# Cross-attention kernel with two layers: context rows of five units normalised on GpSimd, one context block loaded earlier, ternary weights made in the first pass

## The chip, the cores and the metric

The kernel runs on one core of a Trainium2 chip. The metric is the device time of one execution in microseconds (us). Five engines work side by side, each with its own instruction stream and tied to the others by semaphores alone: PE (TensorE, matmuls), DVE (VectorE), ACT (ScalarE), POOL (GpSimd) and SP (SyncE), which here issues every DMA.

## What is computed

Eight batch elements, each with 56 query rows of width 128 and 1500 context rows of width 128; 16 heads of width 8.

```python
q = _ln(latents); x = latents + _mha(q, q)                 # self-attention
kv = _ln(tokens)                                           # tokens = ctx_1024, layernormed
x = x + _mha(_ln(x), kv)                                   # cross-attention, layer 0
x = _fuse_moe(x)                                           # 8 experts, top 2
# layer 1: cross-attention on the context as it is, with ternary weights
gamma = mean(|W|); Wq = clip(round(W / (gamma + 1e-5)), -1, 1) * gamma
x = x + softmax(q @ k.T * SCALE) @ v @ bit_quant(Wo).T + bo
```

## The kernel before, in words

The work is a self-attention, then pass 0 (cross-attention of layer 0), the router and the experts, then pass 1 (cross-attention of layer 1). A pass has eight **units**, one per batch element, and eight **windows**, one per unit. Window n has 12 steps (STEPS). In it PE does the scores of unit n (L1149), the score tiles of unit n+1 (and in window 0 six of its own) whose row maxima DVE takes (`reduce_tile`, L791), the values (L1185), the keys of unit n+2 (`project_k`, L1091, steps 0 to 2), the values' projection of unit n+1 (`project_v`, L1101, steps 4 to 6) and, in pass 0 for n = 0 to 4, the transposes of the normalised context of unit n+3 (`transpose_ctx`, L1080, steps 9, 10, 11). The order of the work is written out by hand, and every engine keeps to its own order.

**Score tiles.** A tile is one 96x112 by 96x500 matmul (L1170) into one of two banks, and DVE reduces it over its 500 columns (L791). PE may begin tile j only when DVE has reduced tile j-2 (`wait(pe, sm_red, n.count(TILES, j + 1 - banks))`). STEP_TILES puts 3, 3, 3, 2, 2, 2, 2, 2, 1, 1, 2, 1 tiles into the steps of a window.

**Context of pass 0.** A block of 1500 context rows is loaded by SP into one of two buffers `cx` (`load_ctx`, L332), as 125 partitions by 12 chunks by 128. In window n DVE takes the statistics of unit n+3 (`ctx_stats`, L763, three chunks in each of steps 1 to 4, the first behind a wait for the load), in step 5 it aggregates them (`ctx_aggregate`, L770 and L773), POOL raises the variance to the power -0.5 (`ctx_rstd`, L464), and in steps 7, 8 and 9 DVE normalises four chunks each in place (`ctx_normalise`, L779: a TENSOR_SCALAR with a mean and a factor per partition). PE transposes chunk by chunk in steps 9 to 11, one third at a time, behind `cn_ready`. Units 0, 1 and 2 have these steps before window 0.

**The keys' split.** ACT writes kf and the first bf16 part (L564, L565), POOL the rest (`k_rest`, L471), DVE the second part (L786), POOL the third (L476). POOL's window is `k_parts(n + 2)` with `ctx_rstd(n + 3)` at its end. SP restacks the parts into kst (`restack`, L378, 6 DMAs for each half).

**SP's queue.** Ahead of window 0: `load_ctx` of units 0, 1 and 2, both halves of `restack(u0)`, the weights of experts 0 and 1 (L351, L352), `load_qall(0)` (L360: 6 DMAs, each behind the part of the split queries it carries), `shift(u0, 0)` (L385), `restack(u1, 0)`. Window n: `load_ctx(n+3)`, `restack(n+1, 1)`, `shift(n, 1)`, `restack(n+2, 0)`, `shift(n+1, 0)`. `load_ctx(n)` waits for the transposes of unit n-2 (`xt_full`).

**The start of pass 0 on DVE.** `split_q(0)` (L749 to L757), then the ternary weights (L936 to L951: 12 TENSOR_SCALAR-like instructions and two whole-tile ones, 128 partitions each), then `start_pass(0)`, whose first instruction is `place_q(u0, 0)` (L815), behind a wait for all six qall DMAs. Pass 1 has the same start without the ternary weights. `place_q` comes again in step 1 and in step 10 of every window. The weights' result (`wq_ready`) is first used by PE after window 7 of pass 0.

Of the kernel before, what the change touches and what calls it, by code (L numbers as in the profile page):

```python
# [26 lines left out]
ALU = mybir.AluOpType  # L27
# [5 lines left out]
B, L, D, T = 8, 56, 128, 1500  # L33
H, DH = 16, 8
E, DFF = 8, 512
EPS = 1e-5
# [14 lines left out]
HSTEP = STEPS // 2  # L51
TPAD = KC * (NCH - 1) + 128
THIRD = T // 3
CPT = NCH // 3
# [95 lines left out]
def build_kernel(nc, x_in, ctx_in, ctxT_in, watt_in, vec_in, rows_in, rwT_in, w1T_in, w2T_in, b2_in,  # L150
                 ident_in, mask_in, out):
    with ExitStack() as ctx:
# [21 lines left out]
        watt = sb("watt", [128, 3, 4, 128])  # L174
# [24 lines left out]
        cmv = sb("cmv", [KC, NCH, 2])  # L199
# [121 lines left out]
        def _(sp):  # L321
# [5 lines left out]
            def load_ctx(n):  # L327

                if n.it is not None or n.c >= 2:
                    sp.wait_ge(xt_full, (n + -2).count(3, 3))  # L330
                src = ctx_in[bass.ds(n.u, 1)].rearrange("a (p c) d -> (a p) c d", c=NCH)
                sp.dma_start(cx[n.par][:], src).then_inc(ld_ctx[n.par], 16)  # L332
# [17 lines left out]
            def load_expert(e, j):  # L350
                sp.dma_start(w1s[j], w1T_in[bass.ds(e, 1)].rearrange("a i f -> (a i) f")).then_inc(ld_exp[j], 16)  # L351
                sp.dma_start(w2s[j], w2T_in[bass.ds(e, 1)].rearrange("a f c d -> (a f) c d")).then_inc(ld_exp[j], 16)  # L352
# [29 lines left out]
            def shift(n, half):  # L382

                sp.wait_ge(mx_evac, n.count(2, half + 1))
                sp.dma_start(qst[n.par][SROWS:KROWS, 4 * half:4 * half + 4, :], mrow[:, half, :]  # L385
                             ).then_inc(shift_loaded[half][n.par], 16)

            def window(n):
                if n.s == 0 and (n + 3).exists():
                    load_ctx(n + 3)  # L390
                if (n + 1).exists():
                    restack(n + 1, 1)
                shift(n, 1)
                if (n + 2).exists():
                    restack(n + 2, 0)
                if (n + 1).exists():
                    shift(n + 1, 0)
                if n.s == 1 and (n + 3).exists():
                    load_xT(n + 3)

# [2 lines left out]
            load_ctx(Unit(0, None, 2))  # L403
            restack(u0, 0)
            restack(u0, 1)
            load_expert(0, 0)
            load_expert(1, 1)
            load_qall(0)
# [28 lines left out]
        @block.gpsimd  # L437
        def _(pool):
            nc.gpsimd.memset(half_neg[:], -0.5)
            nc.gpsimd.memset(euler[:], float(np.e))  # L440
            nc.gpsimd.memset(mean_w[:], 1.0 / (D * D))
            nc.gpsimd.memset(ones_rows[:], 1.0)
            nc.gpsimd.memset(ones_row[:], 1.0)
            for s in range(2):
                last = nc.gpsimd.memset(kst[s][0:SROWS, :, T:TPAD], 0.0)
            last.then_inc(padded, 1)

            def spread_q(b):

                pool.wait_ge(sa_q, 1)  # L450
                wait(pool, sa_sm_full, b - 1)
                nc.gpsimd.tensor_tensor(
                    qbd[:, b % 2], q_sa[:, L * b:L * (b + 1)].unsqueeze(1).broadcast_to([128, H, L]),
                    mask[:, 0:H].unsqueeze(2).broadcast_to([128, H, L]), ALU.mult).then_inc(sa_qbd, 1)

            def token_rstd(n):

                pool.wait_ge(xvar_ready, n + 1)
                nc.gpsimd.tensor_tensor(xrstd[:], xvar[:], half_neg[0:TP, 0:TT], ALU.pow).then_inc(xrstd_ready, 1)  # L459

            def ctx_rstd(n):

                pool.wait_ge(cvar_ready, n.count(1, 1))
                nc.gpsimd.tensor_tensor(crstd[:], cvar[:], half_neg[0:KC, 0:NCH], ALU.pow).then_inc(crstd_ready, 1)  # L464

            def k_rest(n, i):

                wait(pool, k3_done, n.count(3, i - 2))
                pool.wait_ge(k_evac, n.count(6, 2 * i + 2))
                c = slice(THIRD * i, THIRD * (i + 1))  # L470
                nc.gpsimd.tensor_tensor(kr[:, c], kf[:, c], ksplit[n.par][:, 0, c], ALU.subtract).then_inc(kr_done, 1)  # L471

            def k_third_part(n, i):
                pool.wait_ge(k2_done, n.count(3, i + 1))
                c = slice(THIRD * i, THIRD * (i + 1))
                nc.gpsimd.tensor_tensor(ksplit[n.par][:, 2, c], kr[:, c], ksplit[n.par][:, 1, c],  # L476
                                        ALU.subtract).then_inc(k3_done, 1)

            def gates_exp():

                pool.wait_ge(gexp_in, 1)
                nc.gpsimd.tensor_tensor(gates[:], euler[:], lg[:], ALU.pow).then_inc(gexp_done, 1)

            def k_parts(n, ln_unit, between=None):
                k_rest(n, 0)
                k_rest(n, 1)
                if between is not None:
                    between()
                k_third_part(n, 0)
                k_rest(n, 2)  # L490
                k_third_part(n, 1)
                k_third_part(n, 2)
                if ln_unit is not None:
                    ctx_rstd(ln_unit)

            def window(n):
                ln_unit = n + 3 if n.s == 0 and (n + 3).exists() else None
                if (n + 2).exists():
                    k_parts(n + 2, ln_unit)

            pool.wait_ge(padded, 1)
            token_rstd(0)
            u0, u1 = Unit(0, None, 0), Unit(0, None, 1)
            pool.wait_ge(ld_mask, 16)
            spread_q(0)
            spread_q(1)
            for i in range(SA_STEPS):
                if i + 2 < B:
                    spread_q(i + 2)
                if i == 0:  # L510
                    ctx_rstd(u0)
                if i == 3:
                    ctx_rstd(u1)
                if i == 8:
                    ctx_rstd(u0 + 2)

                for kind, unit, third in SA_PIECES.get(i - 1, ()):
                    if kind == "k":
                        k_rest(u0, third)
                for kind, unit, third in SA_PIECES.get(i - 3, ()):  # L520
                    if kind == "k":
                        k_third_part(u0, third)
            token_rstd(1)
            k_parts(u1, None)
            run_windows(0, window)
            token_rstd(2)
            v0 = Unit(1, None, 0)
            k_parts(v0, None, gates_exp)
            token_rstd(3)
            k_parts(v0 + 1, None)  # L530
            run_windows(1, window)


# [178 lines left out]
        def _(dve):  # L712
# [119 lines left out]
            def add_projection(n):  # L832
# [2 lines left out]
                nc.vector.tensor_tensor(xt[:], xt[:], PO[0:TP, :].rearrange("p (t d) -> p t d", t=TT), ALU.add  # L835
                                        ).then_inc(x_added, 1)

            def window(n):
                nxt, k_unit = n + 1, n + 2
                ln_unit = n + 3 if n.s == 0 and (n + 3).exists() else None  # L840
# [2 lines left out]
                for k in range(STEPS):  # L843
# [19 lines left out]
                            max_parts(nxt, 0)  # L863
                    if 0 <= k - K_STEP - 1 < 3 and k_unit.exists():
                        k_second_part(k_unit, k - K_STEP - 1)
                    if ln_unit is not None:
                        if k in (1, 2, 3, 4):
                            ctx_stats(ln_unit, range(3 * (k - 1), 3 * k))
                        if k == 5:
                            ctx_aggregate(ln_unit)  # L870
                        if k in (7, 8, 9):
                            ctx_normalise(ln_unit, (k - 7,))

            every = range(NCH)
            u0, u1 = Unit(0, None, 0), Unit(0, None, 1)
# [55 lines left out]
            token_gain(1)  # L931
            split_q(0)


            dve.wait_ge(gam_ready, 1)
            nc.vector.tensor_scalar(thr[:, 0], gam[:], EPS, 0.5, ALU.add, ALU.mult)  # L936
            nc.vector.tensor_scalar(thr[:, 1], gam[:], EPS, -0.5, ALU.add, ALU.mult).then_inc(thr_ready, 1)
            dve.wait_ge(thr_ready, 1)
            for w in range(4):
                nc.vector.tensor_scalar(wt[:, 0, w], watt[:, 2, w], thr[:, 0, w:w + 1], None, ALU.is_gt)  # L940
                last = nc.vector.tensor_scalar(wt[:, 1, w], watt[:, 2, w], thr[:, 1, w:w + 1], None, ALU.is_lt)
            last.then_inc(tern1, 1)
            dve.wait_ge(tern1, 1)
            nc.vector.tensor_tensor(wt[:, 0], wt[:, 0], wt[:, 1], ALU.subtract).then_inc(tern2, 1)
            dve.wait_ge(tern2, 1)
            for w in range(4):
                last = nc.vector.scalar_tensor_tensor(out=wt[:, 1, w], in0=wt[:, 0, w], scalar=gam[:, w:w + 1],
                                                      in1=watt[:, 2, w], op0=ALU.mult, op1=ALU.subtract)
            last.then_inc(tern3, 1)
            dve.wait_ge(tern3, 1)  # L950
            nc.vector.tensor_tensor(watt[:, 2], watt[:, 2], wt[:, 1], ALU.add).then_inc(wq_ready, 1)  # L951

            def start_pass(s):
                first = Unit(s, None, 0)
# [513 lines left out]
```

## Time and profile before

| | us |
|---|---|
| runs shown | 637.69, 639.55, 640.61; median 639.55 |
| profiled execution, its own time | 638.79 |
| its span | 637.0 |
| busy in the span: PE | 544.5 (85%) |
| DVE | 425.6 (67%) |
| ACT | 326.7 (51%) |
| POOL | 152.7 (24%) |
| chain that ended last | PE 45%, DVE 23%, issue 21%, DMA 4%, POOL 3% |

The profile is of one execution; its own time is its span and 1.79 us around it. Busy shares are averages over stages with different limits, so a stage is read by its own rows. "Idle before" in a row of the trace is the time that an engine sat still ahead of the instruction, with what released it. The granted clock of PE is 1.00 at 2.4 GHz and 0.50 at 1.2 GHz.

### The profile page before, as it was taken

What the parts mean: (1) busy time and instruction counts of PE and PEld (TensorE: products, weight loads), DVE (VectorE), ACT (ScalarE), POOL (GpSimd) and SP (SyncE); (2) the same over time, 40 slices, a digit from 0 to 9 for tenths busy, and PEclk for the clock granted to TensorE, in tenths of its full rate; (3) what the DMA queues carried; (4) which work ended last, traced back from release to release, by engine and by line L of the source; (5) the groups of instructions that cost most, each with busy time, mean ns of one, the idle gap of its engine ahead of it and who ended that gap; (6) DMA issues with size and microseconds to landing.
All of it is one profiled execution on the core that took longest, in us unless ns stands there. A gap on an engine that the chain in (4) does not pass through costs nothing.

```text
span 637.0 us, 16158 instructions
## 1 busy us (share of the span) xinstructions
PE 544.5 (85%) x6582; PEld 383.9 (60%) x6582; DVE 425.6 (67%) x1090; ACT 326.7 (51%) x495; POOL 152.7 (24%) x128
## 2 busy tenths in 40 slices
PE   0699838589999999999967989468999999999996
PEld 0587515266766667676745767234666767667674
DVE  5667478679998999977224302569787687786730
ACT  0165214356666576765743333215566567676573
POOL 1554212313241524300015100223041240421000
PEclk9899668889999999999997989878999999999998
DMA  5010733434436353342200642026536436353300
GB/s 154 32 50 1 164 92 69 126 88 110 132 74 172 72 139 75 75 99 50 100 1 1 170 108 66 9 84 146 137 80 175 121 77 168 88 137 75 74 3 15
DMA packets 25338, 57.44 MB, mean 90 GB/s; under 512 B 4660, under 2 KB 8876, under 8 KB 25268
## 3 DMA queue, kind: packets, MB, share of 16 engines
q1 hardware_dynamic: 25268, 56.45, 34.6%
q8 instruction: 51, 0.84, 0.5%
q14 instruction: 19, 0.16, 0.1%
HBM read 17.81 MB, written 0.23 MB: 28 GB/s over the span
## 4 chain that ended last, share of the span: by engine, by line
PE 45%; DVE 23%; issue 21%; DMA 4%; POOL 3%; ACT 2%; SPq 2%; DVEq 0%; POOLq 0%; ACTq 0%
DVE mxp L791 11%; PE SM L1170 10%; PE PO L1185 9%; PE ST L1149 6%; PE MI L1101 6%; DMA cx<-in_ctx 3%; PE MI L1091 3%; DVE cx L779 3%; DVE qst L815 2%; PE MI L1125 2%; PE SM L1257 2%; DVE ksplit L786 1%; DVE cstat L763 1%; PE SM L1125 1%; DVE xn L732 1%
## 5 line engine op out<-in xcount | busy, mean ns | idle before, releaser
L791 DVE TENSOR_REDUCE mxp<-SM 112x1 f32<-112x500 f32 x364 | 235.2, 673 | 60.5 <-PE SM L1170 59.1
L593 ACT ACTIVATE PT<-ST 128x896 f32<-128x896 f32 x192 | 171.1, 911 | 49.7 <-PE ST L1149 49.1
L1170 PE MATMUL SM<-kst,qst 96*112 96x500 bf16 x364 | 143.1, 407 | 24.7 <-DVE mxp L791 24.1
L1149 PEld LDWEIGHTS ST<-qst,kst 98*128 98x128 bf16 x1536 | 95.0, 100 | 32.6 <-issue 9.7
L1149 PE MATMUL ST<-qst,kst 98*128 98x112 bf16 x1536 | 108.5, 215 | 1.2 <-DMA qst<-mrow 1.2
L471 POOL TENSOR_TENSOR kr<-kf,ksplit 128x500 f32<-128x500 f32 x48 | 56.1, 1170 | 184.4 <-ACT ksplit L565 184.3
L1185 PE MATMUL PO<-PT,vaug 125*32 125x112 f32 x3072 | 96.5, 264 | 2.1 <-ACT PT L593 1.5
L1170 PEld LDWEIGHTS SM<-kst,qst 96*112 96x112 bf16 x364 | 46.8, 131 | 66.9 <-DVE mxp L791 55.2
L1185 PEld LDWEIGHTS PO<-PT,vaug 125*32 125x32 f32 x3072 | 70.5, 110 | 24.5 <-issue 14.9
L577 ACT ACTIVATE vaug<-MI 125x512 f32<-125x512 f32 x48 | 28.7, 598 | 79.4 <-PE MI L1101 79.4
L476 POOL TENSOR_TENSOR ksplit<-kr,ksplit 128x500 bf16<-128x500 f32 x48 | 54.5, 1135 | 53.4 <-DVE ksplit L786 53.4
L1101 PE MATMUL MI<-watt,xT 128*125 128x128 f32 x384 | 56.9, 294 | 0.1
L1101 PEld LDWEIGHTS MI<-watt,xT 128*125 128x125 f32 x384 | 49.1, 197 | 8.9 <-issue 5.0
L564 ACT ACTIVATE kf<-MI,vec 128x500 f32<-128x500 f32 x42 | 28.5, 678 | 40.0 <-PE MI L1091 40.0
L1091 PE MATMUL MI<-xT,watt 128*128 128x500 f32 x84 | 45.9, 629 | 0.0
L699 ACT ACTIVATE moe<-ST,vec 128x448 f32<-128x448 f32 x32 | 20.1, 634 | 35.5 <-PE ST L1368 35.0
L1379 PEld LDWEIGHTS SM<-moe 128*112 128x112 f32 x256 | 31.9, 181 | 9.8 <-issue 8.9
L1023 DVE SCALAR_TENSOR_TENSOR xt<-SM,gates,xt 112x128 f32<-112x128 f32 x32 | 9.0, 343 | 40.4 <-PE SM L1379 40.4
L459 POOL TENSOR_TENSOR xrstd<-xvar,half_neg 112x4 f32<-112x4 f32 x4 | 4.0, 1010 | 127.1 <-DVE xvar L729 127.1
L1368 PE MATMUL ST<-hT,moe 128*128 128x448 f32 x64 | 31.0, 590 | 2.2 <-DMA moe<-in_w2T 2.2
L1379 PE MATMUL SM<-moe 128*112 128x128 f32 x256 | 32.6, 276 | 0.0
L779 DVE TENSOR_SCALAR cx<-cx,cmv,crstd 125x128 f32<-125x128 f32 x96 | 28.6, 366 | 2.7 <-POOL crstd L464 2.7
(129 smaller groups left out, 555.4 us busy)
## 6 DMA issues: line engine op xcount, KB each, us to landing
kst<-ksplit SPq DMA_DIRECT2D x192, 187.5 KB, 3.8
cx<-in_ctx SPq DMA_DIRECT2D x8, 750.0 KB
xT<-in_ctxT SPq DMA_DIRECT2D x8, 750.0 KB, 4.6
moe<-in_w1T SPq DMA_DIRECT2D x8, 256.0 KB, 2.9
moe<-in_w2T SPq DMA_DIRECT2D x8, 256.0 KB, 3.3
qall<-qsplit SPq DMA_DIRECT2D x12, 112.0 KB, 2.3
watt<-in_watt SPq DMA_DIRECT2D x1, 768.0 KB, 5.8
qst<-mrow SPq DMA_DIRECT2D x32, 1.8 KB
```

The source lines that it names most:

```text
L471: nc.gpsimd.tensor_tensor(kr[:, c], kf[:, c], ksplit[n.par][:, 0, c], ALU.subtract).then_inc(kr_done, 1)
L476: nc.gpsimd.tensor_tensor(ksplit[n.par][:, 2, c], kr[:, c], ksplit[n.par][:, 1, c], ALU.subtract).then_inc(k3_done, 1)
L593: nc.scalar.activation(PT[:, k % PTB], ST[:, k % 2, :, 0:4 * PC], ACT.Exp, scale=SCALE).then_inc(exp_done, 1)
L779: last = nc.vector.tensor_scalar(cx[n.par][:, c], cx[n.par][:, c], cmv[:, c, 0:1], crstd[:, c:c + 1], ALU.subtract, ALU.mult)
L791: nc.vector.tensor_reduce(mxp[:, j // 3, j % 3:j % 3 + 1], tile_bank(j, banks), AX.X, ALU.max).then_inc(sm_red, 1)
L1091: mm(bank[:, 0:THIRD], watt[:, n.s + 1, 1], xT[n.par][:, THIRD * i:THIRD * (i + 1)], start=True, stop=True).then_inc(kp_full, 1)
L1101: last = mm(MI[0:KC, D * c:D * (c + 1)], xT[n.par][:, at:at + KC], watt[:, n.s + 1, 2], start=True, stop=True)
L1149: last = mm(ST[:, k % 2, cc, PC * p:PC * (p + 1)], kst[n.par][:, 4 * half + p, at:at + 128], qst[n.par][:, 4 * half + p], start=True, stop ...
L1170: mm(tile_bank(j, banks), qst[n.par][0:SROWS, j // 3], kst[n.par][0:SROWS, j // 3, at:at + THIRD], start=True, stop=True).then_inc(sm_full, 1)
L1185: last = mm(PO[32 * p:32 * p + 32, PC * half:PC * (half + 1)], vaug[n.par][:, c, at:at + 32], PT[0:KC, k % PTB, cc, PC * p:PC * (p + 1)], ...
L1368: mm(ST[:, c // 2, c % 2, 0:N], w1s[j][:, D * c:D * (c + 1)], hT[:], start=True, stop=True).then_inc(fc1_full, 1)
L1379: last = mm(SM[0:TP, j, D * t:D * (t + 1)], h1[:, c, TP * t:TP * (t + 1)], w2s[j][:, c], start=(c == 0 and t == 0), stop=(c == CPE - 1), s ...
```

## The change

1. For units 3 to 7, the 12 normalising TENSOR_SCALARs leave DVE (steps 7, 8, 9 of windows 0 to 4) and go to POOL, right behind `ctx_rstd` of the same unit. In step 5 DVE now waits, before it overwrites the statistics, until POOL has normalised the unit before (units 4 to 7).
2. `load_ctx(n+4)` stands at the end of SP's window n, where `load_ctx(n+3)` stood at the head of window n, and `load_ctx` of unit 3 goes ahead of the experts' weights and of `load_qall(0)`.
3. The ternary weights go from the start of pass 0 to window 5 of pass 0, on DVE behind step 6 and ahead of step 7.

```diff
@@ SP @@
             def window(n):
-                if n.s == 0 and (n + 3).exists():
-                    load_ctx(n + 3)
                 if (n + 1).exists():
                     restack(n + 1, 1)
                 shift(n, 1)
                 if (n + 2).exists():
                     restack(n + 2, 0)
                 if (n + 1).exists():
                     shift(n + 1, 0)
+                if n.s == 0 and (n + 4).exists():
+                    load_ctx(n + 4)
...
             load_ctx(Unit(0, None, 2))
             restack(u0, 0)
             restack(u0, 1)
+            load_ctx(Unit(0, None, 3))
             load_expert(0, 0)
             load_expert(1, 1)
             load_qall(0)
@@ POOL @@
+            def ctx_normalise(n):
+                pool.wait_ge(crstd_ready, n.count(1, 1))
+                for i in range(3):
+                    for c in range(CPT * i, CPT * (i + 1)):
+                        last = nc.gpsimd.tensor_scalar(cx[n.par][:, c], cx[n.par][:, c], cmv[:, c, 0:1],
+                                                       crstd[:, c:c + 1], ALU.subtract, ALU.mult)
+                    last.then_inc(cn_ready, 1)
             def window(n):
                 ln_unit = n + 3 if n.s == 0 and (n + 3).exists() else None
                 if (n + 2).exists():
                     k_parts(n + 2, ln_unit)
+                if ln_unit is not None:
+                    ctx_normalise(ln_unit)
@@ DVE, in the loop over the steps k of a window @@
+                    if n.s == 0 and n.c == B - 3 and k == HSTEP:
+                        ternary_weights()
                     if ln_unit is not None:
                         if k in (1, 2, 3, 4):
                             ctx_stats(ln_unit, range(3 * (k - 1), 3 * k))
                         if k == 5:
+                            if ln_unit.it is not None or ln_unit.c > 3:
+                                dve.wait_ge(cn_ready, (ln_unit + -1).count(3, 3))
                             ctx_aggregate(ln_unit)
-                        if k in (7, 8, 9):
-                            ctx_normalise(ln_unit, (k - 7,))
@@ DVE, between split_q(0) and start_pass(0) @@
-            (the ternary weights, L935 to L951, now in ternary_weights())
```

## Rows read from the trace of the kernel before

**Rows 1.** Busy time by stretch: from, to, length, each engine; then PEclk, DMA share, GB/s.

```profile
111.92:151.06 39.14, 30.29 (x364) 20.91 (x363) 29.00 (x85) 18.56 (x29) 8.90 (x8) 0.87 0.46 122
436.85:464.90 28.05, 25.69 (x352) 17.06 (x352) 23.53 (x48) 17.10 (x26) 7.12 (x7) 1.00 0.60 146
151.06:166.57 15.51, 14.33 (x193) 10.19 (x191) 14.61 (x48) 9.19 (x14) 8.10 (x7) 1.00 0.31 73
166.57:178.90 12.33, 11.91 (x176) 8.54 (x175) 11.13 (x30) 9.65 (x16) 1.36 (x2) 1.00 0.61 163
490.45:505.38 14.93, 14.18 (x193) 10.15 (x191) 11.50 (x24) 9.07 (x14) 6.37 (x6) 1.00 0.35 81
505.38:515.99 10.61, 10.45 (x164) 7.14 (x163) 8.29 (x18) 7.60 (x13) 0.39 (x1) 1.00 0.70 184
```

**Rows 2.** Timeline of DVE in window 0 of pass 0: start, duration, idle before.

```profile
121.02 0.68 DVE L763 BATCH_NORM_STATS2 cstat<-cx 125x6 f32<-125x128 f32 x3 [5.51 <-DMA cx<-in_ctx]
```

**Rows 3.** Timeline of SP's queue, 60 to 190 us and 404 to 420 us.

```profile
76.55 0.99 SPq L351 DMA_DIRECT2D moe<-in_w1T  x1
86.24 3.78 SPq L360 DMA_DIRECT2D qall<-qsplit  x6
109.32 0.78 SPq L332 DMA_DIRECT2D cx<-in_ctx  x1
...
412.06 3.78 SPq L360 DMA_DIRECT2D qall<-qsplit  x6
```

**Rows 4.** Timeline of DVE at the starts of pass 0 and of pass 1.

```profile
87.88 0.16 DVE L936 TENSOR_SCALAR thr<-gam 128x4 f32<-128x4 f32 x1
92.35 0.46 DVE L815 TENSOR_SCALAR qst<-qall,member 96x224 bf16<-96x224 bf16 x2
...
417.65 0.46 DVE L815 TENSOR_SCALAR qst<-qall,member 96x224 bf16<-96x224 bf16 x2 [3.88 <-DMA qall<-qsplit]
```

**Rows 5.** Stretches as in rows 1: SP's queue running dry, and the end of a context load.

```profile
82.00:84.00 2.00, 1.07 (x5) 0.59 (x6) 0.74 (x1) 0.00 (x0) 0.00 (x0) 0.90 0.16 60
118.00:120.00 2.00, 0.00 (x0) 0.00 (x0) 0.00 (x0) 0.00 (x0) 0.52 (x1) 1.00 0.31 121
```

**Rows 6.** Timeline of PE in window 1 of pass 0: first and third group of transposes.

```profile
169.99 0.59 PE L1080 MATMUL MI<-ident,cx 125*128 125x125 f32 x4
...
173.79 0.59 PE L1080 MATMUL MI<-ident,cx 125*128 125x125 f32 x4
```

**Rows 7.** Timeline of POOL, window 1 and start of window 2 of pass 0.

```profile
165.27 2.27 POOL L464 TENSOR_TENSOR crstd<-cvar,half_neg 125x12 f32<-125x12 f32 x1 [4.30 <-DVE cvar L773]
178.51 1.13 POOL L471 TENSOR_TENSOR kr<-kf,ksplit 128x500 f32<-128x500 f32 x1 [10.97 <-ACT ksplit L565]
```

**Rows 8.** Groups of POOL by line and shape: busy, mean ns, idle before.

```profile
L471 POOL TENSOR_TENSOR kr<-kf,ksplit 128x500 f32<-128x500 f32 x48 | 56.1, 1170 | 184.4 <-ACT ksplit L565 184.3
...
L452 POOL TENSOR_TENSOR qbd<-qf,mask 128x896 f32<-128x896 f32 x8 | 13.5, 1688 | 22.0 <-PE SM L1257 12.5 <-DVE qf L885 9.5
...
L441 POOL MEMSET mean_w<- 128x128 f32 x1 | 0.2, 204 | 0.0
```

**Rows 9.** Timeline of DVE in window 5 of pass 0, steps 6 to 8.

```profile
277.43 0.68 DVE L791 TENSOR_REDUCE mxp<-SM 112x1 f32<-112x500 f32 x1 [1.51 <-PE SM L1170]
278.53 1.87 DVE L791 TENSOR_REDUCE mxp<-SM 112x1 f32<-112x500 f32 x3 [0.42 <-PE SM L1170]
```

**Rows 10.** Timeline of PE in the same steps.

```profile
279.26 0.42 PE L1170 MATMUL SM<-kst,qst 96*112 96x500 bf16 x1 [0.16 <-DVE mxp L791]
```

**Rows 11.** PE after an idle time among the experts (timeline); two stretches at low clock (as rows 1).

```profile
372.45 3.60 PE L1368 MATMUL ST<-hT,moe 128*128 128x448 f32 x6 [2.19 <-DMA moe<-in_w2T]
...
122.30:131.50 9.20, 8.82 (x70) 6.17 (x71) 5.79 (x15) 2.56 (x4) 2.27 (x2) 0.51 0.02 8
373.70:377.00 3.30, 3.30 (x10) 2.05 (x9) 0.00 (x0) 1.87 (x3) 0.00 (x0) 0.51 0.01 2
```

**Rows 12.** Timeline of DVE at the start of window 2 of pass 0.

```profile
178.82 1.08 DVE L815 TENSOR_SCALAR qst<-qall,member 96x224 bf16<-96x224 bf16 x2
```

More of the change, by code:

```diff
@@ L836, in add_projection, with ternary_weights @@
                                         ).then_inc(x_added, 1)
+            def ternary_weights():
+                dve.wait_ge(gam_ready, 1)
+                nc.vector.tensor_scalar(thr[:, 0], gam[:], EPS, 0.5, ALU.add, ALU.mult)
+                nc.vector.tensor_scalar(thr[:, 1], gam[:], EPS, -0.5, ALU.add, ALU.mult).then_inc(thr_ready, 1)
+                dve.wait_ge(thr_ready, 1)
+                for w in range(4):
+                    nc.vector.tensor_scalar(wt[:, 0, w], watt[:, 2, w], thr[:, 0, w:w + 1], None, ALU.is_gt)
+                    last = nc.vector.tensor_scalar(wt[:, 1, w], watt[:, 2, w], thr[:, 1, w:w + 1], None, ALU.is_lt)
+                last.then_inc(tern1, 1)
+                dve.wait_ge(tern1, 1)
+                nc.vector.tensor_tensor(wt[:, 0], wt[:, 0], wt[:, 1], ALU.subtract).then_inc(tern2, 1)
+                dve.wait_ge(tern2, 1)
+                for w in range(4):
+                    last = nc.vector.scalar_tensor_tensor(out=wt[:, 1, w], in0=wt[:, 0, w], scalar=gam[:, w:w + 1],
+                                                          in1=watt[:, 2, w], op0=ALU.mult, op1=ALU.subtract)
+                last.then_inc(tern3, 1)
+                dve.wait_ge(tern3, 1)
+                nc.vector.tensor_tensor(watt[:, 2], watt[:, 2], wt[:, 1], ALU.add).then_inc(wq_ready, 1)
             def window(n):
@@ L932, in _ @@
             split_q(0)
[L935 to L951, printed above, removed]
             def start_pass(s):
```

## The prediction

> **What bounds the kernel now.** I read the share of busy time first, and it only says where to look: PE is busy for 85% of the span and DVE for 67%, over stages that differ. The edits touch three places: the start of pass 0, windows 0 to 4 of pass 0 and window 5. So I cut the timeline at events that both passes have and compared the passes, since a window of pass 1 is one of pass 0 without the context's layernorm. The cuts are `place_q` in step 1 and the transposes back of `on` (L1137, step 7).
>
> Window 1 of pass 0 takes 15.51 + 12.33 = 27.84 us, a middle window of pass 1 14.93 + 10.61 = 25.54 us [rows 1]. PE is busy for 26.24 of the 27.84 us and 24.63 of the 25.54 us. A window is bound by PE, with short waits for DVE in between, although DVE is busy for 25.7 us in pass 0. The layernorm costs 2.30 us of a window: 0.58 in steps 1 to 7 (where DVE takes statistics) and 1.72 in steps 7 to 1 (where it normalises and PE transposes).
>
> Window 0 of pass 0 takes 39.14 us and that of pass 1 28.05 us [rows 1]. DVE stood for 5.51 us until the block of unit 3 had landed [rows 2]: its load was issued at 109.32 us, behind the restack of unit 1's first half [rows 3]. With PE idle, the granted clock then fell, and 9.2 us ran at 0.51 (the 1.2 GHz level) [rows 11].
>
> **Edit 2, the loads.** From unit 4 on the position in SP's queue is the one before: the end of window n is the head of window n+1, with nothing between. Only the load of unit 3 moves, from 109.32 us to about 76.6 us, ahead of the experts' weights [rows 3]. Its condition, the transposes of unit 1, is met by then. It lands some 30 us before DVE asks for it, so the wait goes. What is won: window 0 has 39.14 - 28.05 = 11.09 us more than its twin in pass 1. Of that 2.30 is the layernorm as in window 1, and some 1.0 I leave for statistics, because here DVE has six more tiles and no slack in steps 1 to 3. The rest, 7.8 us (the wait of 5.51 and 2.3 of low clock), goes. Next late is DVE's work in steps 1 to 3, as in pass 1. Bounds: 5.5 (the clock stays low for some other cause) to 9.
>
> The moved load has a price at the start. Behind it stand `load_qall(0)`'s six DMAs, for which DVE's first `place_q` waits. At the end of a context load the DMA share is 0.31 and the rate 121 GB/s [rows 5]: 5 of 16 engines carry it, and 750 KB take them 6.3 us. The queue now runs dry at about 83 us (share 0.16) [rows 5], so those five would be free at about 89 us, as the last of the qall DMAs is issued (86.24 + 3.78 us) [rows 3]. I count it with edit 3.
>
> **Edit 3, the ternary weights.** Taking them from the start looks like 92.35 - 87.88 = 4.47 us of DVE [rows 4]. But `place_q` also waits for qall. In pass 1, where no ternary weights stand there, it begins 417.65 - 412.06 = 5.59 us after the first qall issue, with a wait of 3.88 us [rows 3, 4]; in pass 0 it begins 92.35 - 86.24 = 6.11 us after it. So at most 0.52 us is won, the rest was cover for the DMA. The moved load may take that back: I put -0.2, between -0.5 and +1.5.
>
> In window 5 the 4.47 us stand as one block between the reduces of two tiles, and PE has two banks. The reduce of 277.43 us ends at 278.11, the block at 282.5, the next reduce at 283.2. PE begins the tile after next at 279.26 us, released by just that reduce, now the first of the three at 278.53 us [rows 9, 10]. It would begin at 283.25: +4.0 us. PE runs in order, so the values and scores behind it wait too, and DVE's idle time later in the window gives nothing back. And the clock: an idle time of 2.19 us among the experts was followed by 3.3 us at 0.51, the idle time of window 0 by 9.2 us [rows 11]. At half the clock a stretch loses at most half its length, and window 0 lost about 2.3 of 9.2 us, a quarter: 0.8 to 4.6 us, I take 2.2. Together +6.2 us. Bounds: +1.5 (PE finds other cover) to +8.5.
>
> **Edit 1, the normalising.** Off DVE go 12 instructions a window, but what that gives is what PE waited for them. Of the 1.72 us in steps 7 to 1, PE's three groups of transposes take 1.3 (0.59 us each, overlapping the next by some 0.15) [rows 6] and stay. Left is 0.4 us a window, five windows: -2.0 us. Bounds 0 and -3.
>
> On POOL, 12 TENSOR_SCALARs of 125x128 come behind the power, which ends at 165.27 + 2.27 = 167.54 us [rows 7]. PE wants the first third at 169.99 and the last at 173.79 us [rows 6], 173.4 once the 0.4 is gone. So one may take (173.4 - 167.54) / 12 = 0.49 us. No row shows it. From below: a 128x128 MEMSET at 204 ns. From above: a line through the two TENSOR_TENSORs, 1170 ns at 500 columns and 1688 at 896, which gives 0.68 us at 128 columns [rows 8]. The 500-column one scaled by columns gives 0.30. This one reads one tensor, not two, and so stands nearer to that; I take 0.35 us, 4.2 us for twelve, ready at 171.7 us: hidden, with 1.7 us to spare. At 0.68 us it is 2.3 us late a window. POOL's next work begins at 178.51 us [rows 7], so neither the keys' split nor DVE's new wait in step 5 is reached.
>
> **The sum**, against the profiled execution (638.79 us: span 637.0 and 1.79 around it): -7.8 - 0.2 + 6.2 - 2.0 = -3.8, that is 635.0 us. It is 0.76 below the median of the runs shown, so 635.7 us.
>
> **A page that speaks against edit 1.** `place_q` on DVE took 1.08 us for two at 178.82 us, while POOL worked from 178.51 to 179.64 [rows 7, 12]; a pair elsewhere takes 0.46 [rows 4]. The Trainium skill, Perfetto Trace Analysis, section Optimizing Scalar/DVE Operations, says that work moved between GpSimd and VectorE may not help as they share an SBUF port; this row agrees for `place_q`. By it edit 1 would give nothing, 637.7 us; the sum keeps its 2.0, because what DVE runs in steps 6 to 9 are reduces that read PSUM.
>
> **The rivals.** (a) Window 5 is cheap: PE's stall stays 4.0 but the clock holds (633.5), or DVE's block is covered (629.5). For it: PE is dense around it. Against: the two rows on the clock. Chance 0.2. (b) Slower than before: POOL's instruction price becomes the bound. Place: the transposes in steps 9 to 11 of five windows. At 0.68 us each is 12 x 0.68 - 5.86 = 2.3 us late, +11.5: 647.2 us. It outweighs the rest from 5 x (12p - 5.86) = 3.8, p = 0.55 us. For it: the line through the two rows; against: one input, and the small MEMSETs that show little fixed cost. Chance 0.15, half of it between 0.49 and 0.6 us, near no change. (c) DVE finds no relief, by POOL's share of the port: 637.7 us, chance 0.1. (d) The moved load holds back qall by 1.5 us or the clock stays low in window 0: 638 us. Chance 0.1. (e) The change does not do what it says, the block of unit 3 still lands late: it needs only the transposes of unit 1, far behind by then; with edit 3's price it would end 4 us above before. Chance 0.02. The forecast has 0.43.
>
> **The numbers.** Some 0.5% (3.2 us) is what a measurement of this kernel can tell from no change: faster means below 636.3 us. Most of the forecast's own spread (633 to 638) lies below, and (a) all of it: 0.57. Within: the forecast's upper part, (c), (d) and the middle of (b): 0.3. Slower: 0.13. The range 630 to 640.5 leaves out the fully covered window 5 and (b) beyond 0.57 us.
>
> **What would show it.** Right: no wait of DVE for `cx` in window 0, which takes 31 us; clock 1.00 from about 111 us on; windows 1 to 4 at 27.4 us; `place_q` at 5.6 to 6.5 us after the first qall issue; in window 5 an idle time of PE of 4 us behind the ternary weights and a stretch at 0.5 after it; POOL's TENSOR_SCALAR near 0.35 us. Wrong: PE waiting in L1080 for POOL in steps 9 to 11, or a window 5 as long as before.

## The result, and the profile after

| | us |
|---|---|
| before, median of 4 runs | 640.08 (637.69 to 642.92) |
| changed kernel, median of 4 runs | 666.39 (660.20 to 667.74) |
| ratio, 95% interval | 1.039 (1.031 to 1.047) |
| profiled execution: its own time, span | 667.74, 665.9 |
| busy in the span | PE 559.8 (84%), DVE 412.2 (62%), POOL 200.2 (30%) |

The change costs 3.9%, where 0.6% less was forecast. 666.39 us lies outside the range given (630 to 640.5). Now and then an execution runs at a lower clock and takes some per cent longer; the ratios leave such a one out, here a single one (652.43 us, of the kernel with edit 1 undone), which only that kernel's median counts.

Busy time by stretch of the changed kernel, columns as in rows 1. Each of the first four is a window (0, 1, 2 and 5), from its `place_q` of step 1 to the next window's; the fifth is a piece of window 2.

```profile
115.68:151.36 35.68, 30.31 (x364) 20.65 (x363) 26.70 (x72) 18.56 (x28) 17.91 (x20) 0.88 0.49 118
151.36:184.25 32.89, 28.03 (x367) 19.64 (x366) 23.05 (x65) 19.00 (x29) 18.90 (x20) 0.95 0.37 95
184.25:218.25 34.00, 29.14 (x367) 20.39 (x366) 23.05 (x65) 19.09 (x29) 18.89 (x20) 0.90 0.37 92
286.41:317.35 30.94, 25.80 (x352) 18.07 (x350) 24.02 (x57) 16.15 (x24) 6.46 (x6) 0.89 0.25 57
...
209.50:216.50 7.00, 5.98 (x49) 4.07 (x50) 1.84 (x6) 2.17 (x4) 0.87 (x2) 0.52 0.72 166
```

DVE's busy time in a window fell from 25.7 to 23.05 us, as the edit meant, and the window went from 27.84 [rows 1] to 34.00 us. The two profiled spans, cut at events that both have, differ so:

| stretch | before | after | difference |
|---|---|---|---|
| start to the first qall issue | 86.24 | 87.90 | +1.66 |
| to the first `place_q` | 6.11 | 7.97 | +1.86 |
| to window 0, step 1 | 19.57 | 19.81 | +0.24 |
| window 0 | 39.06 | 35.68 | -3.38 |
| windows 1 to 4 | 111.72 | 135.05 | +23.33 |
| window 5 | 24.79 | 30.94 | +6.15 |
| the rest | 349.51 | 348.55 | -0.96 |
| span | 637.0 | 665.9 | +28.9 |

The first line is no effect of the change: its code ahead of that point is the one before but for one DMA issued at 78.65 us, and the other kernels, with or without that DMA, show 85.87 to 88.62 us.

POOL in window 2, its timeline (start, duration, count), answering to rows 7:

```profile
198.56 2.29 POOL L465 TENSOR_TENSOR crstd<-cvar,half_neg 125x12 f32<-125x12 f32 x1 [4.31 <-DVE cvar L785]
200.95 9.42 POOL L502 TENSOR_SCALAR cx<-cx,cmv,crstd 125x128 f32<-125x128 f32 x12
```

Twelve instructions take 9.42 us, 0.785 us each. PE in the same window, its timeline:

```profile
204.23 0.62 PE L1096 MATMUL MI<-ident,cx 125*128 125x125 f32 x4 [0.78 <-POOL cx L502]
...
207.42 0.62 PE L1096 MATMUL MI<-ident,cx 125*128 125x125 f32 x4 [1.06 <-POOL cx L502]
...
210.52 1.07 PE L1096 MATMUL MI<-ident,cx 125*128 125x125 f32 x4 [1.66 <-POOL cx L502]
...
212.68 1.72 PE L1201 MATMUL PO<-PT,vaug 125*32 125x112 f32 x32
```

Each third of the transposes waits for POOL, 3.5 us in all; in window 0 it is some 2 us (16.0 us over the five windows). POOL's longer work holds up nothing else: its next instruction, for the keys' split, began after 7.58 us of idle time, and DVE did not stand in step 5. With the third wait the four transposes take 1.07 us where they took 0.62, and the values behind them 1.72 us: the clock has fallen to the 1.2 GHz level, and 7 us run at 0.52.

Window 5, PE's timeline around the ternary weights, answering to rows 10:

```profile
302.26 0.56 PE L1165 MATMUL ST<-qst,kst 98*128 98x112 bf16 x8
306.94 0.67 PE L1186 MATMUL SM<-kst,qst 96*112 96x500 bf16 x1 [4.12 <-DVE mxp L803]
307.54 1.72 PE L1201 MATMUL PO<-PT,vaug 125*32 125x112 f32 x32
```

An idle time of 4.12 us, and low clock behind it. At the start DVE's first `place_q`, and what SP issued ahead of it (timelines of DVE and SP, answering to rows 4 and 3):

```profile
95.87 0.46 DVE L827 TENSOR_SCALAR qst<-qall,member 96x224 bf16<-96x224 bf16 x2 [6.24 <-DMA qall<-qsplit]
```

```profile
78.65 0.83 SPq L332 DMA_DIRECT2D cx<-in_ctx  x1
...
87.90 3.77 SPq L360 DMA_DIRECT2D qall<-qsplit  x6
```

DVE waits 6.24 us for the qall DMAs: the 4.47 us of ternary weights that covered such a wait are gone, and the DMAs land later, 7.97 us after the first issue where the start of pass 1 showed 5.59.

### The profile page after: what moved, and what is told of

Same layout as the page of the kernel before. It is cut to its first block, busy times and chain, and to the rows that moved or that the text cites. A ratio compares the mean times of both kernels' runs of the same rounds, so it can differ in the third digit from the quotient of the medians.

```text
span 665.9 us, 16158 instructions
## 1 busy us (share of the span) xinstructions
PE 559.8 (84%) x6582; PEld 395.7 (59%) x6582; DVE 412.2 (62%) x1030; ACT 328.1 (49%) x495; POOL 200.2 (30%) x188
## 4 chain that ended last, share of the span: by engine, by line
PE 44%; issue 20%; DVE 18%; POOL 11%; DMA 3%; ACT 1%; SPq 1%; DVEq 0%; ACTq 0%; POOLq 0%
DVE mxp L803 9%; PE SM L1186 9%; PE PO L1201 8%; POOL cx L502 7%; PE ST L1165 6%; PE MI L1117 5%; PE MI L1107 4%; POOL crstd L465 2%; PE MI L1141 2%; DVE qst L827 2%; PE SM L1273 2%; DMA cx<-in_ctx 2%; DVE ksplit L798 1%; PE MI L1096 1%; DVE cstat L775 1%
## 5 line engine op out<-in xcount | busy, mean ns | idle before, releaser
L1186 PE MATMUL SM<-kst,qst 96*112 96x500 bf16 x364 | 145.6, 415 | 20.9 <-DVE mxp L803 20.5
L1165 PEld LDWEIGHTS ST<-qst,kst 98*128 98x128 bf16 x1536 | 96.9, 102 | 34.6 <-issue 11.9
L1165 PE MATMUL ST<-qst,kst 98*128 98x112 bf16 x1536 | 110.6, 217 | 1.1 <-DMA qst<-mrow 1.1
L1201 PE MATMUL PO<-PT,vaug 125*32 125x112 f32 x3072 | 100.7, 271 | 2.1 <-ACT PT L605 1.5
L1201 PEld LDWEIGHTS PO<-PT,vaug 125*32 125x32 f32 x3072 | 74.0, 113 | 25.7 <-issue 17.3
L1107 PE MATMUL MI<-xT,watt 128*128 128x500 f32 x84 | 49.0, 668 | 0.0
L502 POOL TENSOR_SCALAR cx<-cx,cmv,crstd 125x128 f32<-125x128 f32 x60 | 47.0, 799 | 0.5
L1395 PEld LDWEIGHTS SM<-moe 128*112 128x112 f32 x256 | 31.2, 177 | 9.3 <-issue 8.3
L564 ACT ACTIVATE xT<-MI,vec 128x500 f32<-128x500 f32 x24 | 18.4, 767 | 31.5 <-PE MI L1096 31.5
L1096 PE MATMUL MI<-ident,cx 125*128 125x125 f32 x96 | 17.4, 312 | 18.1 <-POOL cx L502 16.0
```

What stands on the lines that cost most here:

```text
L502: last = nc.gpsimd.tensor_scalar(cx[n.par][:, c], cx[n.par][:, c], cmv[:, c, 0:1], crstd[:, c:c + 1], ALU.subtract, ALU.mult)
L1107: mm(bank[:, 0:THIRD], watt[:, n.s + 1, 1], xT[n.par][:, THIRD * i:THIRD * (i + 1)], start=True, stop=True).then_inc(kp_full, 1)
L1165: last = mm(ST[:, k % 2, cc, PC * p:PC * (p + 1)], kst[n.par][:, 4 * half + p, at:at + 128], qst[n.par][:, 4 * half + p], start=True, stop ...
L1186: mm(tile_bank(j, banks), qst[n.par][0:SROWS, j // 3], kst[n.par][0:SROWS, j // 3, at:at + THIRD], start=True, stop=True).then_inc(sm_full, 1)
L1201: last = mm(PO[32 * p:32 * p + 32, PC * half:PC * (half + 1)], vaug[n.par][:, c, at:at + 32], PT[0:KC, k % PTB, cc, PC * p:PC * (p + 1)], ...
L1395: last = mm(SM[0:TP, j, D * t:D * (t + 1)], h1[:, c, TP * t:TP * (t + 1)], w2s[j][:, c], start=(c == 0 and t == 0), stop=(c == CPE - 1), s ...
```

## The experiments

The kernel before was measured again beside each group of kernels, and every ratio is against those runs. What was open: whether POOL's price, the time of one of its instructions, made the windows long (theory P), or the moved load (L), or the ternary weights (S), and what the low clock adds.

**Edit 1 undone.** The changed kernel with the normalising back on DVE, and without DVE's wait in step 5.

```diff
-                if ln_unit is not None:
-                    ctx_normalise(ln_unit)
...
                             ctx_aggregate(ln_unit)
+                        if k in (7, 8, 9):
+                            ctx_normalise(ln_unit, (k - 7,))
```

> The changed kernel with the normalising of units 3 to 7 back on DVE (edit 1 undone, edits 2 and 3 kept). Theory P (POOL's price of 0.79 us an instruction makes the transposes late, and the idle time drops the clock): windows 1 to 4 return from 33 to 34 us to 27.9 us, window 0 to about 31 us, window 5 stays near 31 us; 638 us (636 to 641). Rival L (what costs is the moved load, through the DMA queue and the clock at the start): it stays above 655 us. Rival S (the ternary weights in window 5 are the larger loss): above 650 us.

Measured: 641.63 us (median of ten), ratio 1.002 (1.000 to 1.005). The stretches of windows 0, 1 and 5:

```profile
114.41:146.96 32.55, 28.58 (x364) 19.66 (x365) 29.24 (x84) 19.00 (x29) 9.56 (x8) 0.95 0.54 131
146.96:174.80 27.84, 26.25 (x367) 18.74 (x366) 25.76 (x77) 18.84 (x29) 9.45 (x8) 1.00 0.45 114
258.33:288.96 30.63, 25.51 (x352) 17.98 (x350) 24.00 (x56) 16.13 (x24) 6.46 (x6) 0.89 0.28 66
```

Without edit 1 nearly the whole loss is gone; window 1 is back at 27.84 us. L and S fall. What stays above the expected 638 us is the start, where the first `place_q` comes 10.2 us after the first qall issue (7.97 in the changed kernel), and window 0, with 32.55 us where about 31 were expected.

**Edit 1 alone**, on the kernel before (`ctx_normalise` on POOL behind `ctx_rstd`, the wait in step 5, nothing else).

> The kernel before with edit 1 alone: late load, ternary weights at the start. Theory P: windows 1 to 4 at 33 to 34 us as in the changed kernel (+23), window 0 some 3 to 5 us longer than before; 667 us (663 to 672). Rival L: near 642 us. Rival S: near 640 us.

Measured: 664.54 us, ratio 1.037 (1.034 to 1.040). Windows 1 to 4 take 34.33 and three times 34.13 us. Theory P stands: the time lies within its expected range, the windows a little above theirs. Window 0 took 40.44 us, 1.4 longer than before, less than expected.

**Edit 2 alone**, on the kernel before.

```diff
...
-                if n.s == 0 and (n + 3).exists():
-                    load_ctx(n + 3)
...
+                if n.s == 0 and (n + 4).exists():
+                    load_ctx(n + 4)
...
             restack(u0, 1)
+            load_ctx(Unit(0, None, 3))
             load_expert(0, 0)
```

> The kernel before with edit 2 alone. Theory P and the forecast's account of edit 2: the wait of 5.5 us and 2.3 us of low clock in window 0 go, -7.8; the first place_q comes 8.0 us after the first qall issue where it was 6.1, +1.9; the ternary weights lie beside that wait; 634.2 us (632 to 637). Rival L: at or above 645 us.

Measured: 636.11 us, ratio 0.994 (0.992 to 0.996). The stretches of window 0 and of a piece in it:

```profile
115.11:147.67 32.56, 28.59 (x364) 19.75 (x365) 29.16 (x85) 19.02 (x29) 9.95 (x8) 0.95 0.52 126
...
123.50:127.00 3.50, 3.50 (x46) 2.74 (x44) 2.25 (x7) 0.92 (x1) 1.61 (x2) 0.52 0.00 0
```

Window 0 lost 6.5 of its 39.06 us, not 7.8: PE still waits for DVE in steps 1 to 3 (0.50, 0.75 and 1.07 us), and 3.5 us run at low clock. The first `place_q` came 8.57 us after the first qall issue, +2.5, and DVE stood 2.38 us for the qall DMAs although the ternary weights lay beside them.

**Edit 3 alone**, on the kernel before (`ternary_weights()` in window 5 behind step 6).

> The kernel before with edit 3 alone. By the forecast: +4.1 us of idle PE in window 5 and 2 to 3 us of low clock behind it, -0.5 at the start; 645.8 us (644 to 648). Rival S: above 652 us. Rival C (other work covers it): 640 us.

Measured: 646.98 us, ratio 1.012 (1.008 to 1.016). Window 5 took 30.94 us where it took 24.79; PE stood for 4.12 us, and 7 us ran at low clock (timeline of PE, then a stretch):

```profile
281.63 0.66 PE L1174 MATMUL SM<-kst,qst 96*112 96x500 bf16 x1 [4.12 <-DVE mxp L791]
282.22 1.72 PE L1189 MATMUL PO<-PT,vaug 125*32 125x112 f32 x32
...
279.50:286.50 7.00, 4.87 (x55) 3.42 (x59) 4.05 (x9) 1.41 (x2) 0.00 (x0) 0.51 0.00 0
```

The first `place_q` came 5.55 us after the first qall issue, 0.56 us earlier than before. That is all that taking the ternary weights from there gives.

The three parts alone sum to +3.7 - 0.6 + 1.2 = +4.3%, their whole is +3.9% (3.1 to 4.7).

**The load behind qall.** Edit 2 (its other lines as above) with the load of unit 3 further back in SP's queue, behind the experts' weights and qall.

```diff
...
             load_expert(1, 1)
             load_qall(0)
+            load_ctx(Unit(0, None, 3))
             shift(u0, 0)
```

> The kernel before with edit 2 alone, but the load of unit 3 behind the six qall DMAs in SP's queue, not ahead of the experts' weights. Theory Q (the moved load holds back qall, 2 to 4 us at the start): the first place_q comes again 6.1 us after the first qall issue, window 0 stays at 32.6 us as with the load moved early; 2 to 3 us below that kernel, 633.5 us. Rival: the start is longer for another cause (the state of the clock), then 636 us as with the early load.

Measured: 635.19 us, ratio 0.991 (0.988 to 0.993). The load was issued at 89.69 us, the first `place_q` came 6.11 us after the first qall issue, as before, and window 0 took 32.55 us. In the profiled executions the early load's 2.5 us at the start are gone. The intervals of the two ratios overlap (0.988 to 0.993 and 0.992 to 0.996), so the whole times alone do not settle it; the time of `place_q` does. All profiles agree: 5.55 to 6.11 us after the first qall issue in the seven kernels without the early load, 7.97 to 10.22 us in the five with it. DMA share at the start, this kernel and the changed one, as rows 5:

```profile
84.00:86.00 2.00, 0.69 (x2) 0.00 (x0) 1.20 (x3) 0.00 (x0) 0.00 (x0) 0.82 0.03 8
86.00:88.00 2.00, 0.00 (x0) 0.00 (x0) 1.90 (x7) 0.00 (x0) 0.00 (x0) 0.50 0.32 78
```

```profile
84.00:86.00 2.00, 1.11 (x2) 0.50 (x2) 0.74 (x1) 0.00 (x0) 0.00 (x0) 0.50 1.06 234
86.00:88.00 2.00, 0.72 (x1) 0.00 (x0) 1.17 (x3) 0.00 (x0) 0.00 (x0) 0.50 0.64 157
```

In the changed kernel the first qall DMA is issued at 87.90 us, and the share just before it is 0.64. In this kernel it is issued at 85.87 us, and the share just before it is 0.03.

**Ternary weights in window 7.** As the last kernel, with edit 3's call under another condition.

```diff
+                    if n.s == 0 and n.c == B - 1 and k == BACK_STEP:
+                        ternary_weights()
```

> As the kernel with the load behind qall, and the ternary weights behind step 3 of window 7 of pass 0, where DVE stood idle for 3.9 and 11.9 us. Theory: nothing waits for them there; the first place_q comes 5.6 us after the first qall issue where it was 6.1; 633.0 us, no difference from the kernel without that edit that can be measured. Rival: PE stalls or the clock falls in window 7 as it did in window 5, then 637 us or more.

Measured: 634.25 us, ratio 0.990 (0.987 to 0.993). The first `place_q` came 5.59 us after the first qall issue, and DVE was still idle for 7.42 us behind the ternary weights. They are free there, and the move is worth nothing that these runs can tell (ratio 0.991 without it).

**POOL on half the columns.** The changed kernel; of units 3 to 7 columns 64 to 127 are left as loaded.

```diff
-                        last = nc.gpsimd.tensor_scalar(cx[n.par][:, c], cx[n.par][:, c], cmv[:, c, 0:1],
+                        last = nc.gpsimd.tensor_scalar(cx[n.par][:, c, 0:64], cx[n.par][:, c, 0:64], cmv[:, c, 0:1],
```

> The changed kernel with POOL normalising only 64 of the 128 columns of each chunk (the other half of units 3 to 7 is left as loaded). It splits POOL's 0.79 us into a fixed part and a part by columns. If it goes by columns: 0.42 us, in time for PE, windows 1 to 4 at 27.5 us, 642 us (edit 3 and the late qall stay). If it is fixed: 0.75 us, 34 us a window, 665 us. By the line through POOL's two-input rows (1.3 ns a column): 0.71 us, some 1 us less lateness a window, 660 us.

Measured: 646.76 us, ratio 1.010 (1.006 to 1.013). POOL's timeline, PE's in the same window, and the stretch of window 2:

```profile
163.50 6.76 POOL L502 TENSOR_SCALAR cx<-cx,cmv,crstd 125x64 f32<-125x64 f32 x12
```

```profile
170.41 0.62 PE L1096 MATMUL MI<-ident,cx 125*128 125x125 f32 x4 [0.82 <-POOL cx L502]
```

```profile
175.46:204.12 28.66, 26.38 (x367) 18.66 (x366) 23.09 (x66) 18.85 (x29) 16.24 (x20) 1.00 0.43 109
```

None of the three guesses: 6.76 / 12 = 0.563 us. With 0.785 at 128 columns a straight line through the two points gives 3.5 ns a column and 0.34 us fixed. At 0.563 PE waits once, for 0.82 us, the clock stays up, and the window is 28.66 us. Even at half the columns POOL is late for the last third.

**A third on POOL.** The load behind qall, DVE normalising two thirds and POOL the last, with a semaphore of its own.

```diff
+                for c in range(CPT * 2, CPT * 3):
+                    last = nc.gpsimd.tensor_scalar(cx[n.par][:, c], cx[n.par][:, c], cmv[:, c, 0:1],
+                                                   crstd[:, c:c + 1], ALU.subtract, ALU.mult)
+                last.then_inc(cn_pool, 1)
...
-                        if k in (7, 8, 9):
+                        if k in (7, 8):
```

> As the kernel with the load behind qall, with only the last third of each of units 3 to 7 (4 of 12 instructions) on POOL and the other two thirds on DVE as before. POOL's four take 3.2 us and end about 3 us before PE wants them. It shows what DVE's relief gives where POOL is in time. If PE's small wait ahead of the third transposes was DVE's: 0.2 to 0.4 us a window, 1 to 2 us in all, 632 us. Rival (DVE was not the bound there, or POOL's share of the port slows DVE): no difference or +1 us.

Measured: 633.20 us, ratio 0.987 (0.984 to 0.990). Stretches of windows 1 and 2, then POOL's and DVE's timelines in window 1:

```profile
142.69:170.42 27.73, 26.22 (x367) 18.62 (x366) 24.94 (x74) 18.66 (x29) 13.73 (x12) 1.00 0.44 112
170.42:198.06 27.64, 26.25 (x367) 18.67 (x366) 24.95 (x74) 18.76 (x29) 13.76 (x12) 1.00 0.46 115
```

```profile
159.47 4.28 POOL L502 TENSOR_SCALAR cx<-cx,cmv,crstd 125x128 f32<-125x128 f32 x4
```

```profile
160.37 1.25 DVE L791 TENSOR_SCALAR cx<-cx,cmv,crstd 125x128 f32<-125x128 f32 x4
```

With POOL in time the window falls by 0.1 to 0.2 us, from 27.85. So little was there to win. The whole time fell by 2.0 us against the kernel with the load behind qall, as the upper end expected, but not for the reason given: in the profiled executions window 0 took 30.49 us and not 32.55, because the clock did not fall in it (mean 1.00 against 0.95). Why it did not is open: PE's waits for DVE there were 0.35, 0.90 and 1.07 us, and 0.50, 0.75 and 1.08 us in the kernel where it fell.

**PE kept busy.** The changed kernel with one more fp32 matmul ahead of each third of transposes, into the bank that these overwrite.

```diff
                 misc_free(prev)
+                if n.c >= 3:
+                    mm(MI[:, 0:N], watt[:, 0, 0], hT[:], start=True, stop=True)
                 pe.wait_ge(cn_ready, n.count(3, i + 1))
```

> The changed kernel with one more matmul ahead of each third of transposes of units 3 to 7, into the bank that the transposes then overwrite (fp32, 448 columns, some 0.8 us at full clock). It fills PE's idle time there and adds nothing where PE waits longer than that. Theory K (half of the loss of a window is the clock: 7 us at 0.5 behind 3.5 us of idle time in three pieces): the granted clock stays at 1.00 in windows 1 to 4 and these take 31 us, not 34; some 654 us. Rival (the lateness alone makes the window long, the low clock lies in time that PE would wait anyway): 34 us or more a window, 666 us or more.

Measured: 657.38 us, ratio 1.029 (1.025 to 1.032). The stretch of window 2 and PE's timeline in window 1:

```profile
179.06:210.28 31.22, 29.20 (x373) 19.56 (x372) 23.08 (x66) 18.94 (x29) 18.86 (x20) 1.00 0.40 101
```

```profile
173.97 0.65 PE L1098 MATMUL MI<-ident,cx 125*128 125x125 f32 x4 [0.58 <-POOL cx L502]
```

More work on PE, and the kernel is faster than the changed one: the clock stays at 1.00 in windows 1 to 4, and each takes 31.2 us, not 34.0. (The intervals of the two ratios, 1.025 to 1.032 and 1.031 to 1.047, just overlap; the stretches do not.) So of the 6.2 us that a window lost, about 3.4 are PE waiting for POOL and 2.8 the clock that this waiting brought down.

**The parts together**, each where it has cover: a third on POOL, the load behind qall, the ternary weights in window 7.

> The last third on POOL, the load of unit 3 behind the qall DMAs, and the ternary weights behind step 3 of window 7: the three parts of the change, each where the runs showed cover for it. First place_q 5.6 us after the first qall issue, windows 1 to 4 at 27.7 us, window 7 unchanged: 0.5 us below the kernel with the last third on POOL, 632.7 us. Rival: another loss of the start shows in its place, no difference.

Measured: 633.14 us, ratio 0.988 (0.986 to 0.990). No difference from the kernel with a third on POOL. Window 0 took 34.09 us here, at a mean clock of 0.89. These two versions beat both the kernel before (by 1.2 to 1.3%) and the changed one; most of that (0.9%) is edit 2 with the load behind qall.

## Why the prediction was wrong

**The step that failed is POOL's price.** "I take 0.35 us" for one TENSOR_SCALAR of 125x128; it is 0.785. So the term that was put at nothing, "hidden, with 1.7 us to spare", became 3.5 us of waiting in each of windows 1 to 4. The price lies above the upper bound of 0.68 us too. That bound was a line through two other instructions, 1.3 ns a column and 0.52 us fixed; the measured line has the smaller fixed part, 0.34 us, and nearly three times the slope, 3.5 ns. The two instructions read two tensors each and do one operation; this one reads one tensor, does two operations and takes a scalar per partition for each. Which of these makes the slope no run separates. The Trainium skill, GPSIMD Engine Reference, section 4.1 Engine selection, says that with one input POOL runs roughly at line rate; the trace does not agree: 3.5 ns a column and 0.34 us fixed, where DVE takes 0.256 us for the whole instruction (1.02 us for four, in the chain that ended last in the kernel before).

**The rule around it was right.** "One may take 0.49 us": 12 x 0.785 - 5.86 = 3.56 us late, and PE waited 3.50. At 0.563 us the rule gives 0.9, and PE waited 0.82. Rival (b) named the place and the point from which it decides. But it was given 0.15, and its 647 us were short twice: in the price, and in the clock, which I had counted for window 5 and left out here. Three waits of 0.78, 1.06 and 1.66 us brought the clock down as one of 4 us does; the kernel with the busy PE shows it. The case of a price far above the bound had no place in the range.

**Edit 1's gain** was put at 0.4 us a window. With a third on POOL 0.1 to 0.2 showed, and the relief of a whole move was never seen alone; that PE and not DVE bound the window is right. Rival (c), DVE's relief lost to the shared port, did not decide: in windows 1 to 4 of the changed kernel `place_q` took 0.48 us beside POOL's normalising, where it took 0.46 before, and with a third on POOL the window fell.

**Edit 2.** The wait for the block went, as forecast. Window 0 fell by 6.5 us with edit 2 alone and not by 7.8, since the low clock went only in part; where the clock did not fall, with a third on POOL, window 0 took 30.49 us, 8.6 less than before. The account of SP's queue was right in kind and wrong in size: I had the five engines free just in time, and the first `place_q` came 1.9, 2.5 and 4.1 us later, counted from the first qall issue, in the changed kernel, with edit 2 alone and with edit 1 undone. The bound was +1.5. That spread between kernels that are alike at this point is not explained.

**Edit 3** went as forecast: +6.15 us in window 5 against 6.2, with 4.12 us of idle PE against 4.0, and 0.56 us at the start against 0.52. Rival (a), window 5 cheap, is out.

**Rival (e)**: the edit of the loads does move only one load. The block was in time: DVE did not wait for `cx` in window 0.

With the price 0.785 in the sum, the lateness of 3.56 us over five windows alone would have given 635.7 + 17.8 = 653.5 us, and with 2.8 us of clock a window 667.5. That this comes so near to 666.39 is in part luck. It counts 6.4 us for window 0, where 3.1 showed (35.68 against 32.55 us with edit 1 undone); against that stand 1.3 us that edit 2 gave less there and 2.1 us more at the first `place_q`.

## What to carry to other kernels

Before work goes to another engine, time that very instruction on it, and set it against the slack: the time until the latest end that its reader allows, divided by the count. A line through other instructions is no bound: it was 0.68 us, and 0.785 was measured. And ask what the offloading can win at most: DVE was busy for 92% of these windows, and taking a third of the normalising off it gave 0.1 to 0.2 us a window.

In these windows the waits of PE that let the clock fall cost their length and half to four fifths of it again (6.15 us for 4.12, 6.2 for 3.4); three short waits did as much as one long one. Work whose removal looks like a gain (the ternary weights) may lie beside the wait for a DMA, and the block of 4.47 us cost PE 4.12 us between two tiles of a loop with two banks, and nothing that can be measured where its engine was idle.

## What the runs showed of the hardware

- POOL's TENSOR_SCALAR with two operations, fp32, 125 partitions: 0.785 us from one to the next at 128 columns, 0.563 at 64; DVE's takes 0.256 at 128.
- A granted clock of 1.00 stayed there with one wait of 0.82 us for POOL in a window; behind waits of 0.78, 1.06 and 1.66 us it was 0.52 for 7 us, and 0.51 around one of 4.12 us.
- Where DVE's and POOL's TENSOR_SCALARs ran at the same time, POOL's four took 4.28 us and not 3.14 (4 x 0.785), and DVE's first four 1.25 us and not 1.11. The Trainium skill, SBUF — State Buffer, section Who interferes with whom, says that a tensor_scalar of VectorE can run in a mode with two ports, and that of such an instruction and a GpSimd one the first to issue holds the shared ports for its whole length and the other fully blocks. The trace agrees that the two slow each other, but not that DVE is blocked for a whole instruction of POOL: its four lost 0.14 us together, where one of POOL's takes 0.785. `place_q`, a TENSOR_SCALAR too, took 0.48 us beside POOL's normalising, 0.46 without it, and 1.08 beside POOL's TENSOR_TENSOR.
- With a context load ahead of them in SP's queue, issued 8 to 10 us earlier, the qall DMAs let `place_q` begin 7.97 to 10.22 us after the first of them was issued; without it, where DVE stood waiting for them, this was 5.55 to 5.61 us. So they landed 2.4 to 4.6 us later. The DMA share at 84 to 88 us was 1.06 and 0.64 in the changed kernel against 0.03 and 0.32 with the load behind qall.
